# Key and value rows of 2048 bytes, the weights behind the values, and the former sums scaled in two operations

## The reference

```
x = layernorm(x + messages(x, edge vectors, edge lengths))        # linear maps, sum over the edges of a receiver
xn = layernorm(x) * g + b
q, k, v = xn @ Wq + bq, xn @ Wk + bk, xn @ Wv + bv                # 8 heads of 32
ep = edge_features @ We + be
score[e, h] = sum_d q[dst, h, d] * (k[src, h, d] + ep[e, d]) / sqrt(32) * edge_weight[e]
m[n, h] = max of score over the edges of receiver n
ex = exp(score - m[dst]);  s = sum of ex over the edges of a receiver
out[n, h, :] = sum over the edges of (ex / s) * v[src, h, :]
x = x + alpha * (out @ Wo + bo)
x = x + beta * (gelu(layernorm(x) * g2 + b2 @ W1 ...) @ W2 + b2)  # feed-forward, 256 -> 1024 -> 256
result = layernorm(x_in + x)
```

## Time and profile before

| | |
|---|---|
| median of 3 timed runs | 2524.44 us (2523.85 to 2524.78) |
| span of the profiled execution | 2736.8 us |
| VectorE busy | 2183.1 us, 80% |
| TensorE busy | 2107.6 us, 77% |
| GpSimd busy | 1618.3 us, 59% |
| ScalarE busy | 1524.3 us, 56% |
| attend, first L1745 to last L1752 | 1415.1 to 2671.0 us |

### The profile page before, as it was taken

One profiled execution on the slowest core, in us unless ns is written; L12 is line 12 of the kernel. 1 busy time (PEld: TensorE's weight loads), 2 busy tenths in 40 slices (PEclk: granted clock), 3 DMA queues, 4 the chain that ended last, 5 costly groups with the idle time before them and its releaser, 6 DMA issues. The chain is left out here.

```text
span 2736.8 us, 41806 instructions
## 1 busy us (share of the span) xinstructions
PE 2107.6 (77%) x9647; PEld 1611.0 (59%) x9647; DVE 2183.1 (80%) x3415; ACT 1524.3 (56%) x4291; POOL 1618.3 (59%) x1808
## 2 busy tenths in 40 slices
PE   3999999999999999679815666666566666656666
PEld 2787878777777777533314455455455545545555
DVE  6888888888888888645546878878888788878793
ACT  5787888788877887433223444444444444444443
POOL 5666666666666666342246666666666666666642
PEclk8999999999999999889957788878878878887787
DMA  6232222222222222769856666666666666666651
GB/s 203 72 84 81 83 83 83 83 82 84 83 83 81 84 82 84 167 165 253 234 181 168 168 173 175 173 165 173 177 169 175 169 172 176 167 175 170 173 141 45
DMA packets 157414, 379.08 MB, mean 139 GB/s; under 512 B 47810, under 2 KB 63298, under 8 KB 157186
## 3 DMA queue, kind: packets, MB, share of 16 engines
q0 software_dynamic: 100544, 309.00, 40.6%
q1 hardware_dynamic: 44946, 68.53, 8.7%
q10 hardware_dynamic: 11904, 1.34, 0.4%
HBM read 353.36 MB, written 37.07 MB: 143 GB/s over the span
## 5 line engine op out<-in xcount | busy, mean ns | idle before, releaser
L1358 POOL DMA_INDIRECT kv_e<-kv_rows,edge x752 | 716.9, 953 | 408.4 <-issue 223.4
L487 POOL DMA_INDIRECT feat<-in_x_rows,idx x664 | 677.1, 1020 | 236.2 <-issue 234.8
L523 ACT ACTIVATE vsh<-feat,rec_a 128x256 f32<-128x256 f32 x1980 | 806.8, 495 | 8.9 <-DMA feat<-in_x_rows,idx 4.8
L1541 PE MATMUL ps_sum<-kv_e,ident 128*128 128x264 f32 x1504 | 473.8, 477 | 376.9 <-issue 264.2
L1541 PEld LDWEIGHTS ps_sum<-kv_e,ident 128*128 128x128 f32 x1504 | 352.5, 240 | 481.8 <-issue 283.6
L571 PE MATMUL ps_a<-msg,hot 128*128 128x257 f32 x1312 | 409.4, 393 | 4.0 <-issue 4.0
L573 PE MATMUL ps_a<-msg,hot 128*128 128x256 f32 x1312 | 390.6, 379 | 0.1
L575 PE MATMUL ps_a<-msg,hot 128*128 128x192 f32 x1312 | 320.2, 325 | 0.0
L573 PEld LDWEIGHTS ps_a<-msg,hot 128*128 128x128 f32 x1312 | 248.6, 190 | 38.2 <-issue 1.9
L575 PEld LDWEIGHTS ps_a<-msg,hot 128*128 128x128 f32 x1312 | 248.8, 190 | 34.9
L571 PEld LDWEIGHTS ps_a<-msg,hot 128*128 128x128 f32 x1312 | 222.2, 189 | 66.3 <-issue 66.3
(11 more groups left out here) (419 smaller groups left out, 3182.2 us busy)
## 6 DMA issues: line engine op xcount, KB each, us to landing
ef<-in_ef_t SPq DMA_DIRECT2D x84, 256.0 KB
kv_e<-kv_rows,edge POOLq DMA_INDIRECT x752
rows_e<-rows SPq DMA_DIRECT2D x41, 272.0 KB
feat<-in_x_rows,idx POOLq DMA_INDIRECT x664
rows_e<-in_ef_t SPq DMA_DIRECT2D x1, 7446.0 KB, 26.6
kv_rows<-kv SPq DMA_DIRECT2D x20, 260.0 KB, 2.5
rows_e<-in_ef_t SPq DMA_DIRECT2D x1, 3706.0 KB
x<-x_rows SPq DMA_DIRECT2D x23, 128.0 KB
```

The lines of the kernel that those rows point to most:

```text
L487: pool.indirect_dma_start(out=feat[:, u, c, 0, :, :].rearrange("p a b -> p (a b)"), out_offset=None, in_=g.x_rows, in_offset=bass.Indirect ...
L523: ins = act.activation(vsh[:, u % TURN, c, j, :, :], feat[:, u % TURN, c, 0, :, :], ACT.Copy, scale=rec_a[:, u % 2, c, 1 + j:2 + j])
L1358: pool.indirect_dma_start(out=kv[:, u, s, :], out_offset=None, in_=g.kv_rows, in_offset=bass.IndirectOffsetOnAxis(ap=edge[:, u, s, DH + 1: ...
L1541: mm = pe.matmul(out, g.ident[:], kv[:, u, s, D:], start=(s == 0), stop=False, skip_group_check=True)
```

## The change

- `KV` is 512 numbers: a row of `kv_rows` is 2048 bytes. `SUM` is 264.
- A slot of `kv_e` keeps its 520 numbers: 256 of keys, 256 of values, and 8 weights behind them, which no gather writes. Sums, `kept` and `acc` have the same order: 256 sums of values, then 8 of weights.
- Project: the memset of `kv` goes, and one operation of 512 numbers does what L1137 and L1139 did.
- Attend: ScalarE writes the 8 weights of a slot side by side. VectorE multiplies values that are side by side, and scales the former sums in two operations: first the 8 sums of weights, which have a factor each, then the 256 of values, for which the factor of a head is spread over 32. Each of them raises `v_kept`, and TensorE and ScalarE wait for the second.
- `divide` and its like in Output read the 8 sums of weights side by side.

```diff
-HEAD = DH + 1
-KV = D + HEADS * HEAD
+KV = 2 * D
+SUM = D + HEADS
...
-            dve.memset(kv[:], 0.0).then_inc(p_bias, 1)
...
-            dve.wait_ge(p_bias, 3)
+            dve.wait_ge(p_bias, 2)
...
-                dve.tensor_tensor(kv[:, u, 0:D], ps_kv[:, 0:D], bias[:, D:2 * D], ALU.add)
-                by_head = lambda row: row.rearrange("p (h d) -> p h d", h=HEADS)
-                dve.tensor_tensor(by_head(kv[:, u, D:])[:, :, 0:DH], by_head(ps_kv[:, D:]), by_head(bias[:, 2 * D:]),
-                                  ALU.add).then_inc(p_kv, 1)
+                dve.tensor_tensor(kv[:, u, :], ps_kv[:], bias[:, D:], ALU.add).then_inc(p_kv, 1)
...
-        kv = sb("kv_e", [P, RING, SLOTS, KV])
+        kv = sb("kv_e", [P, RING, SLOTS, D + SUM])
...
-                        out=kv[:, u, s, :], out_offset=None, in_=g.kv_rows,
+                        out=kv[:, u, s, 0:KV], out_offset=None, in_=g.kv_rows,
...
-                weight = kv[:, u, :, D:].rearrange("p s (h d) -> p s h d", h=HEADS)[:, :, :, DH]
+                weight = kv[:, u, :, KV:]
                 act.activation(weight, score[:, u, 0:SLOTS, :], ACT.Exp)
...
-                act.wait_ge(v_kept, k + 1)
+                act.wait_ge(v_kept, k * 2 + 2)
...
-                pe.wait_ge(v_kept, k + 1)
+                pe.wait_ge(v_kept, k * 2 + 2)
                 pe.matmul(out, g.ident[:], kept[:, u % BANKS, :], start=False, stop=True,
                           skip_group_check=True).then_inc(v_sum, 1)
...
-                    vals = kv[:, u, slots, D:].rearrange("p s (h d) -> p s h d", h=HEADS)[:, :, :, 0:DH]
+                    vals = kv[:, u, slots, D:KV].rearrange("p s (h d) -> p s h d", h=HEADS)
...
-                dve.tensor_tensor(by_head(kept[:, u % BANKS, :]), by_head(ps_o[:, (u - 1) % BANKS, 0:HEADS * HEAD]),
-                                  fade[:, u, :].rearrange("p (h d) -> p h d", d=1).broadcast_to([P, HEADS, HEAD]),
+                dve.tensor_tensor(kept[:, u % BANKS, D:], ps_o[:, (u - 1) % BANKS, D:SUM], fade[:, u, :],
                                   ALU.mult).then_inc(v_kept, 1)
+                dve.tensor_tensor(by_head(kept[:, u % BANKS, 0:D]), by_head(ps_o[:, (u - 1) % BANKS, 0:D]),
+                                  fade[:, u, :].rearrange("p (h d) -> p h d", d=1).broadcast_to([P, HEADS, DH]),
+                                  ALU.mult).then_inc(v_kept, 1)
...
-                dve.tensor_scalar(den[:], heads[:, :, DH], TINY, None, ALU.max).then_inc(w_link, 1)
+                dve.tensor_scalar(den[:], g.acc[:, bass.ds(out, 1), D:].rearrange("p a h -> p (a h)"), TINY, None,
+                                  ALU.max).then_inc(w_link, 1)
```

More of the change, by code:

```diff
@@ L1205, in stage_attend @@
         fade = sb("fade", [P, RING, HEADS])
-        kept = sb("kept", [P, BANKS, HEADS * HEAD])
+        kept = sb("kept", [P, BANKS, SUM])
         ps_o = ctx.enter_context(nc.psum_tensor("ps_sum", [P, BANKS, 512], F32))
@@ L1415, in keep @@
                 w = window_of(act, i)
-                act.activation(g.acc[:, bass.ds(w, 1), :].rearrange("p a d -> p (a d)"), ps_o[:, u % BANKS, 0:HEADS * HEAD],
+                act.activation(g.acc[:, bass.ds(w, 1), :].rearrange("p a d -> p (a d)"), ps_o[:, u % BANKS, 0:SUM],
                                ACT.Copy).then_inc(v_acc, 1)
@@ L1536, in step @@
                 pe.wait_ge(v_fade, k + 1)
-                out = ps_o[:, u % BANKS, 0:HEADS * HEAD]
+                out = ps_o[:, u % BANKS, 0:SUM]
                 for half in range(2):
@@ L1789, in divide @@
                 out = done_window(dve, t + 2)
-                heads = g.acc[:, bass.ds(out, 1), :].rearrange("p a (h d) -> p (a h) d", h=HEADS)
+                heads = g.acc[:, bass.ds(out, 1), 0:D].rearrange("p a (h d) -> p (a h) d", h=HEADS)
                 dve.wait_ge(w_res, t + 1)
                 dve.wait_ge(v_acc, t * RING + 1)
-                dve.tensor_scalar(den[:], heads[:, :, DH], TINY, None, ALU.max).then_inc(w_link, 1)
+                dve.tensor_scalar(den[:], g.acc[:, bass.ds(out, 1), D:].rearrange("p a h -> p (a h)"), TINY, None,
+                                  ALU.max).then_inc(w_link, 1)
                 dve.wait_ge(w_link, t * LINKS + 1)
@@ L1797, in divide @@
                 dve.scalar_tensor_tensor(att[:].rearrange("p (h d) -> p h d", h=HEADS),
-                                         heads[:, :, 0:DH], g.has[:, bass.ds(out, 1)],
+                                         heads, g.has[:, bass.ds(out, 1)],
                                          den[:].rearrange("p (h d) -> p h d", d=1).broadcast_to([P, HEADS, DH]),
@@ L2032, in divide @@
                 now = g.acc[:, LAPPED + w, :]
-                heads = now.rearrange("p (h d) -> p h d", h=HEADS)
-                dve.tensor_scalar(den[:], heads[:, :, DH], TINY, None, ALU.max).then_inc(o_den, 1)
+                heads = now[:, 0:D].rearrange("p (h d) -> p h d", h=HEADS)
+                dve.tensor_scalar(den[:], now[:, D:], TINY, None, ALU.max).then_inc(o_den, 1)
                 dve.wait_ge(o_den, w * 2 + 1)
@@ L2039, in divide @@
                 dve.scalar_tensor_tensor(att[:].rearrange("p (h d) -> p h d", h=HEADS),
-                                         heads[:, :, 0:DH], g.has[:, LAPPED + w:LAPPED + w + 1],
+                                         heads, g.has[:, LAPPED + w:LAPPED + w + 1],
                                          den[:].rearrange("p (h d) -> p h d", d=1).broadcast_to([P, HEADS, DH]),
```

## The result

The changed kernel takes 2529.69 us (median of 11 executions, 2526.95 to 2532.58), the kernel before, timed beside it, 2524.44 (11, 2521.04 to 2526.62): +5.25 us, a ratio of 1.0024, 95% interval 1.0016 to 1.0032. The forecast was 2529.1. The sign is resolved; whether it is more than 0.2% is not, since the interval spans that bound. The profiled execution is one of those timed, 2529.69 us with a span of 2527.5, and has none of the 204 us of pauses of the profile of before.

A forecast was written before the change was run, and what follows sets the result against it. VectorE, working in Attend without a pause, was taken to bound the kernel. +6.2 (added instruction), -0.5 (start) and -1.0 (Project) sum to +4.7 us on the median of 2524.44: 2529.1 us, range 2521 to 2537.5.

The forecast's parts named there:

- What bounds the kernel: Attend: without the profile's 204 us of stalls, VectorE works without a pause, 45.14 to 45.54 us a lap of four steps.
- One instruction more per step, +6.2: Attend: the second scaling operation adds only an instruction's fixed cost, 0.066 us in each of 94 steps, +6.2 us.
- The rival of the whole fixed cost: Attend: the short scaling operation pays its whole fixed cost, 0.151 us a step; +13.2 us in all, 2537.6 us; chance 0.14.
- What the start absorbs, -0.5: First steps of Attend: the added time vanishes in VectorE's waits for gathers, -0.5 us, between 0 and -2.
- Project, -1.0: Project: one operation of 512 numbers instead of two of 256 saves 0.066 us in 20 windows; -1.0, between -1.3 and 0.
- Memset: Project: the removed memset was over before VectorE's next operation waited 0.37 us for TensorE, so 0.
- the values' gaps: Attend: multiplying values without gaps between heads takes VectorE as long as with them, so 0.
- rows of 2048 bytes: Attend's gathers: 1.5% fewer bytes save nothing, as GpSimd's time per gather has no bytes in it and DMA has free time; 0.
- The weights: Attend: ScalarE may write the weights faster side by side than in 302 ns, but nobody waits for it; 0.
- Gathers that set the pace: Attend: VectorE waits for GpSimd's gathers every lap, so the added 0.26 us fills idle time; some 2524.5 us; chance 0.16.
- DMA that sets the pace: Attend: DMA engines bound the steps, which shorten by 1.54%; -17.4 us with Project, 2507.0 us; chance 0.08, whole or in part.
- The chances: Whole kernel: slower by over 0.2% (5.05 us) 0.40, within 0.2% 0.49, faster 0.11.

The follow-up runs named there:

- the kernel with spread factors: The changed kernel with ScalarE writing the factors spread out in one tile of 264 numbers, so VectorE scales all sums in one instruction: 2524.03 us, ratio 1.0002.
- the light VectorE: The changed kernel without adding the edge's part to the keys in Attend, and with one scaling by the first head's factor: 2737.7 us against 2748.15, ratio 0.9963.
- the first and the third set: Two of the three sets of four follow-up runs, on two chips where the kernel before takes some 2748 us, with pauses on several engines.

## Why the prediction was right, and where it was off

**What bounds the kernel.** Right: VectorE, in Attend, without a pause. The step that carried it, that the 204 us of stalls are absent from the timed executions, holds: the trace after has none. The reason given, the nearness of two numbers, was thin, and one of them was off. The lap that was taken as undisturbed, 45.14 us, is the last of the 23, and its last step is 0.20 us short in every trace without pauses, as in this one (12.28 for 12.48 in both kernels). A lap out of the middle makes the stalls some 195 us instead of 204, and VectorE's lap 45.35 where the prediction had 45.14 to 45.54.

**One instruction more per step, +6.2.** The mechanism and the size of one are right, by kernels with one, two and three scalings: 0.06 to 0.07 us each, not 0.151. The rival of the whole fixed cost is out, since the second operation starts 0.08 us after the first out of the same PSUM bank. The Trainium skill, VectorE: DVE Perf Modes, section on the TRN2 errata, which charges 120 cycles to an operation out of PSUM, had the added one at an estimated 125 ns and the kernel at 2535.2; here it is 66 ns in a row that doesn't wait. The page's figure comes nearer to the whole duration of a short one, 153 to 163 ns.

The sum over a lap is off. Three steps of a lap grew by 0.06 each, the fourth not: 12.48 in the changed kernel and 12.48 in the kernel before between its pauses. There, in the fourth step, the reduction starts 0.33 us after the operation before it, in the changed kernel 0.26 (the kernel before again, first; then the changed one):

```profile
2398.06 0.23 DVE L1761 SCALAR_TENSOR_TENSOR score<-beyond,score 128x64 f32<-128x64 f32 x1
2398.39 0.28 DVE L1766 TENSOR_REDUCE top<-score 128x8 f32<-128x72 f32 x1
```

```profile
1676.99 0.22 DVE L1757 SCALAR_TENSOR_TENSOR score<-beyond,score 128x64 f32<-128x64 f32 x1
1677.25 0.28 DVE L1762 TENSOR_REDUCE top<-score 128x8 f32<-128x72 f32 x1
```

So 0.07 us that the kernel before lost in that step has gone. It isn't the scaling that took it away. The changed kernel with rows of 2080 bytes, whose stage is the same on VectorE, has the 0.33 again and 12.55 us. The two kernels with one scaling in the new layout have 0.26 there, but start the addition 0.32 us after L1764 or its like instead of 0.20, and have 12.53. With three scalings it is 0.26 and 0.20, and 12.55. Where such a distance is longer, a register instruction of VectorE's own queue comes 0.12 us late, in every lap; where none is, none comes late. Why is open. In the new layout one, two and three scalings make laps of 45.39, 45.54 and 45.81 us, +0.15 and +0.27, and without the 0.12 the first would be an estimated 45.27. So the fourth step pays for an added instruction like the others, 0.27 a lap as the sum had it (0.26). That the change cost only 0.19 (45.54 against 45.35, a lap with 0.07 lost of its own) is luck.

**Laps of 45.8.** The prediction gave 45.4 to 45.8 for a lap as a spread. It is two values: three laps at 45.54 and every fourth at 45.8. Of the 0.28 of that lap 0.24 are in these rows (each a gather of GpSimd and the operation of VectorE that began under it), the rest in L1757, 0.26 to 0.29 instead of 0.22 there:

```profile
1785.59 0.95 POOL L1354 DMA_INDIRECT kv_e<-kv_rows,edge  x1 [0.30 <-issue]
1786.23 0.30 DVE L1791 TENSOR_SCALAR den<-acc 128x8 f32 x1
...
1819.53 0.95 POOL L1354 DMA_INDIRECT kv_e<-kv_rows,edge  x1 [0.30 <-issue]
1820.09 0.50 DVE L1812 TENSOR_SCALAR acc<-y,mv,rstd 128x256 f32 x1
```

L1791 takes 0.16 us, save where it starts 0.64 us after a gather did: five times, each time 0.30. L1812 takes 0.41, and 0.50 to 0.52 in the five laps where it starts 0.54 to 0.56 behind one. At all other distances seen they have their usual length, but for 0.18 once. VectorE's lap falls behind GpSimd's by some 0.3 us, four laps are one distance of gathers (1.257), so they meet every fourth lap. The Trainium skill, SBUF — State Buffer, section SBUF: two separate sides, says that VectorE, in a mode that uses two ports or with two inputs in SBUF (the latter only against a GpSimd instruction that reads SBUF), and GpSimd share a pair of ports as an exclusive lock, which the first holds for its whole instruction while the other fully blocks. The traces agree that they exclude each other, in both directions (0.14 and 0.1 us on VectorE, 0.11 on the gather), but not that it lasts for the whole instruction: a gather takes 0.95 us, and L1791 begun 0.12 to 0.51 us into one takes its usual 0.16. They don't show the port itself. The sum had nothing for it.

The two errors nearly cancel, which is luck as well: 23 laps x 0.19 = 4.4, 5 meetings x 0.28 = 1.4, 5.8 in all, for 6.2. The 0.19 rests on a lap of the kernel before that is put together from steps between pauses; no quiet trace of it shows one.

**What the start absorbs, -0.5.** It is there and smaller: the first lap is 50.20 us in the changed kernel, 50.04 in the same with rows of 2080 bytes and 50.17 with one scaling, so nothing of its 0.26 is seen, and 0.2 to 0.3 us are absorbed. That makes 5.6; measured 5.25, within what the medians can tell.

**Project, -1.0.** Wrong, by nine traces of the pausing chips: 0. The duration was right (672 ns), the saving too (the next operation starts 0.60 us on, 0.66 before), but VectorE isn't on the chain there. Of the two ends that the prediction gave, -1.3 and 0, the second was the true one. On the quick chip, to which the time belongs, it isn't shown: nothing of two operations was profiled there. Without the term the sum is +5.7.

**Memset, the values' gaps, rows of 2048 bytes: 0.** The last two are measured (1214 against 1215 ns; 2529.97 against 2529.69 us, to 2.5 us or so). The memset by itself was not tried; it is back in the kernel with rows of 2080 bytes, which is no slower. **The weights: 0** held too, though their operation got 62 ns shorter.

**The rivals.** Gathers that set the pace: not so, the addition never waits for them after the fourth step, and their lead grows. It was a near thing all the same: GpSimd's bare lap is 45.28, so by estimate no saving on VectorE alone brings the kernel with spread factors more than 23 x 0.11 = 2.5 us; the light VectorE, which was to show it, fell to a pausing chip. DMA that sets the pace: refuted by the wide rows. The chances follow: a sum of +4.7 against a bound of 5.05 was rightly called a toss-up; it fell 0.2 us beyond by the medians.

## What to carry to other kernels

Price one more short instruction on a saturated engine by the distance of starts in a row that doesn't wait, here 0.07 us where its duration is 0.16, and multiply by the steps; then don't put a wait there, which cost some six times as much (1.6 us a lap for 0.27). Don't expect tenths of a microsecond a lap to come out: a late register instruction moved the laps of these kernels by 0.07 to 0.12 us whatever the change. A saving on an engine that doesn't end the stage is nothing, however well the duration is known: look at the time between repeats of the stage before it goes into the sum. Where a profile has large stalls without a releaser, compare another execution's time before any term is taken from them.

## What the runs showed of the hardware

- On two chips (the first and the third set) this one-core kernel takes 2747 to 2748 us instead of 2524, 8.9% more, with the same work; the profile of before, with its span of 2737, is of that kind. TensorE's like products are torn there by 1 to 2.5 us in which it waits for nothing shown, VectorE and ScalarE stand idle in the same stretches, and ScalarE's queue takes 0.7 us for register and branch instructions that take 0.31 at most elsewhere. Why is open.
- A gather under way and a VectorE operation on SBUF alone exclude each other for 0.1 to 0.14 us when they fall at a certain distance; two engines of nearly equal laps keep step by it, GpSimd losing 0.11 us a lap at the same instruction.
- A wait of VectorE for its instruction just before costs 0.11 us where nothing else is queued, and 0.6 to 0.8 us where register work for a later instruction stands behind it.
- An operation of VectorE taken out of a chain of waits, with the semaphore raised by the queue in its place, gave back 0.05 of its 0.26 us.
- In some kernels VectorE's queue handles one register instruction of a lap 0.12 us late, at a place that differs between kernels with the same instructions around it; the step is then 0.07 to 0.12 us longer.
